# Four engines' order tables of a graph network kernel, made anew around VectorE's and GpSimd's shared port

## What is computed

```python
x = _layernorm(x + L0(x))     # adj @ (x @ W) + b
x = _layernorm(x + L1(x))     # (si + sj + adj * w_r + g_b) @ x @ W + b
x = _layernorm(x + L2(x))     # attention: e = sigmoid(a_tgt + a_src + be) * mask; elu twice
x = _layernorm(x + L3(x))     # 5 steps of a gated recurrent unit on adj @ h
```

## Time and profile before

| what | value |
|---|---|
| median of 3 runs (lowest, highest) | 1314.46 us (1313.87, 1315.95) |
| the profiled execution | 1314.02 us |
| its span, first to last instruction | 1312.2 us |
| mean granted clock of TensorE | 0.98 of full speed |
| share of the span: ACT busy | 45% |
| what TensorE does most: line 622, three kinds of matmul on `xh`, `xl` | 656 matmuls of each kind |

### The profile page before, as it was taken

The page is one execution under the profiler, slowest core; times in us unless marked ns, Lnnn a source line. Parts: engine busy times, 40 slices in busy tenths (PEclk is TensorE's granted clock), DMA queues, the critical chain, the costliest instruction groups (busy, mean ns, idle before and its releaser), DMA issues.

```text
span 1312.2 us, 15431 instructions
## 1 busy us (share of the span) xinstructions
PE 1232.6 (94%) x5488; PEld 938.1 (71%) x5488; DVE 921.8 (70%) x2154; ACT 587.1 (45%) x855; POOL 275.3 (21%) x174
## 2 busy tenths in 40 slices
PE   6968889999999999998999999999999999999994
...
DVE  6798767966866676669487666767677767655557
...
PEclk9977999999999999999999999999999999999997
...
DMA packets 38459, 52.70 MB, mean 40 GB/s; under 512 B 2736, under 2 KB 19632, under 8 KB 38384
## 3 DMA queue, kind: packets, MB, share of 16 engines
...
## 4 chain that ended last, share of the span: by engine, by line
PE 77%; DVE 15%; issue 3%; POOL 2%; ACT 2%; DMA 1%; POOLq 0%; SPq 0%; DVEq 0%; ACTq 0%
PE ps L622 41%; PE ps L627 6%; PE ps L629 6%; PE ps L628 6%; PE ps L719 5%; PE ps L633 4%; PE ps L640 3%; DVE x L1046 2%; DVE ring L1168 2%; PE ps L837 2%; DVE tl L1023 1%; PE ps L732 1%; PE ps L681 1%; PE ps L733 1%; PE ps L711 1%
## 5 line engine op out<-in xcount | busy, mean ns | idle before, releaser
L622 PE MATMUL ps<-adj_hi,xh 128*128 128x512 f32 x656 | 284.1, 433 | 4.1 <-DVE xl L1023 2.3
L622 PE MATMUL ps<-adj_hi,xl 128*128 128x512 f32 x656 | 257.1, 392 | 0.0
L622 PE MATMUL ps<-adj_lo,xh 128*128 128x512 f32 x656 | 256.2, 390 | 0.0
L622 PEld LDWEIGHTS ps<-adj_hi,xh 128*128 128x128 f32 x656 | 123.4, 188 | 41.9 <-issue 17.5
L591 POOL TENSOR_TENSOR fr<-fr,ring 128x512 f32<-128x512 f32 x84 | 126.9, 1511 | 104.9 <-DVE ring L1168 101.2
L622 PEld LDWEIGHTS ps<-adj_lo,xh 128*128 128x128 f32 x656 | 123.6, 188 | 34.3 <-issue 12.5
L622 PEld LDWEIGHTS ps<-adj_hi,xl 128*128 128x128 f32 x656 | 123.1, 188 | 27.0
L1168 DVE TENSOR_TENSOR ring<-ring,mk 128x512 f32<-128x512 f32 x128 | 104.7, 853 | 32.3 <-ACT ring L907 31.1
L719 PE MATMUL ps<-ring,fz 128*128 128x512 f32 x224 | 112.2, 610 | 15.8 <-DVE ring L1168 15.8
L1186 DVE TENSOR_TENSOR r<-r,hT 128x512 f32<-128x512 f32 x80 | 62.2, 789 | 92.0 <-ACT r L960 92.0
L863 ACT ACTIVATE mh<-ps 128x512 fp32r<-128x512 f32 x80 | 47.8, 597 | 172.8 <-PE ps L622 172.6
(11 more groups left out here) (272 smaller groups left out, 2486.0 us busy)
## 6 DMA issues: line engine op xcount, KB each, us to landing
mk<-mask_scratch SPq DMA_DIRECT2D x128, 256.0 KB, 2.8
...
```

Of the source, the lines that this page charges most:

```text
L622: mm = pe.matmul(dst, a[:, t, :], b[:, t, cut(h)], start=(t == 0 and i == 0), stop=(t == T - 1 and i == 2))
```

## The change

All instructions stay as they are, and so do the functions that issue them. Only the text of `TABLES` differs: the four orders are made anew, with the condition that in the plan VectorE and GpSimd never hold the SBUF port that they share at the same time. Besides the first stage, units 0, 1, 3, 4, 10 to 18 and 20 to 28 differ. Lines of the same kind are left out below (units 20 to 28 repeat 10 to 18 nearly; ScalarE's and VectorE's slots in those units move with TensorE's).

```diff
--- before.py
+++ after.py
...
     "PE": """
...
-first rows:0 y1a:0 m1b:1 y1b:0 sums:1 rows:1 y1a:1 y1b:1 t2a:0 t2b:0 t2a:1 t2b:1 pja:1 pja:0 pjb:0 pjb:1
-first tha:0 thb:0 tga:0 tgb:0 tha:1 thb:1 tga:1 e00:0 e01:0 e02:0 tgb:1 m1a:2 e03:0 e04:0 e05:0 e06:0 m1b:2
-first e07:0 sums:2 rsa:0 rows:2 y1a:2 rva:0 e10:0 e11:0 e12:0 y1b:2 y2a:0 e13:0 e14:0 e15:0 e16:0 e17:0
-first e00:1 rsb:0 m0a:3 rvb:0 e01:1 e02:1 e03:1 m0b:3 y2b:0 e04:1 e05:1 e06:1 y0a:3 y0b:3 e07:1 t2a:2 t2b:2
-first e10:1 e11:1 e12:1 pja:2 pjb:2
-unit0 @2 e13:1 e14:1 e15:1 tha:2 thb:2 @3 tga:2 tgb:2 e16:1 e17:1 @5 rsa:1 m1a:3 rsb:1 m1b:3 rva:1 sums:3 e00:2 e01:2 rows:3 y1a:3 rvb:1 y1b:3 e02:2 @6 e03:2 @7 y2a:1 e04:2 @8 y2b:1 e05:2 e06:2 @17 e07:2 @19 rsa:2 @21 rva:2 @25 e10:2 y2a:2 e11:2 e12:2 e13:2
-unit1 @10 e14:2 @26 e15:2
+first rows:0 y1a:0 m1b:1 y1b:0 sums:1 rows:1 y1a:1 t2a:0 t2b:0 pja:0 pjb:0 y1b:1 tha:0 thb:0 tga:0 tgb:0
+first m1a:2 m1b:2 e00:0 e01:0 e02:0 sums:2 e03:0 e04:0 e05:0 t2a:1 t2b:1 rows:2 y1a:2 e06:0 e07:0 pja:1
+first y1b:2 rsa:0 rva:0 e10:0 e11:0 pjb:1 e12:0 y2a:0 e13:0 e14:0 e15:0 tha:1 e16:0 thb:1 tga:1 tgb:1 e17:0
+first rsb:0 m0a:3 rvb:0 e00:1 e01:1 e02:1 m0b:3 y2b:0 e03:1 e04:1 e05:1 y0a:3 y0b:3 e06:1 e07:1 t2a:2 t2b:2
+first pja:2 pjb:2 e10:1
+unit0 @1 e11:1 e12:1 @5 e13:1 tha:2 thb:2 @6 e14:1 e15:1 tga:2 tgb:2 @8 e16:1 e17:1 rsa:1 @12 rsb:1 m1a:3 rva:1 m1b:3 rvb:1 sums:3 e00:2 y2a:1 rows:3 y1a:3 y2b:1 e01:2 y1b:3 e02:2 @19 e03:2 @25 e04:2
+unit1 @1 e05:2 e06:2 @2 e07:2 @4 rsa:2 e10:2 e11:2 rva:2 @7 e12:2 @10 y2a:2 @19 e13:2 @22 e14:2 @26 e15:2
...
-unit13 @2 y0b:5 @9 e00:4 e01:4 e02:4 @11 e03:4 e04:4 @14 e05:4 e06:4 @16 e07:4 @18 rsa:4 @20 rva:4 e10:4 e11:4 e12:4 m1a:5 @21 y2a:4 e13:4 @22 e14:4 @23 e15:4 @25 e16:4 @27 e17:4
-unit14 @2 m1b:5 @14 rsb:4 @16 rvb:4 @19 sums:5 @23 y2b:4 @27 rows:5
...
+unit13 @2 m0b:5 tha:4 thb:4 y0a:5 tga:4 tgb:4 @5 y0b:5 @7 e00:4 e01:4 e02:4 @10 e03:4 e04:4 @20 e05:4 e06:4 @21 e07:4 @24 rsa:4 @27 rva:4 e10:4 e11:4 e12:4
+unit14 @7 y2a:4 e13:4 e14:4 e15:4 @8 m1a:5 e16:4 e17:4 @10 rsb:4 @11 m1b:5 @16 rvb:4 @19 sums:5 @23 y2b:4 @27 rows:5
...
-unit17 @2 e00:5 @7 e01:5 e02:5 @9 e03:5 e04:5 e05:5 @12 e06:5 e07:5 @14 rsa:5 e10:5 e11:5 rva:5 e12:5 e13:5 e14:5 @16 y2a:5 e15:5 e16:5 e17:5 @18 rsb:5 @20 rvb:5 @25 y2b:5
-unit18
+unit17 @2 e00:5 @7 e01:5 e02:5 @10 e03:5 e04:5 @18 e05:5 @20 e06:5 e07:5 @23 rsa:5 e10:5 e11:5 rva:5 e12:5 e13:5 e14:5 @25 y2a:5 e15:5 e16:5 @26 e17:5
+unit18 @1 rsb:5 @3 rvb:5 @9 y2b:5
...
-unit27 @1 rsa:7 e10:7 @2 rva:7 @4 e11:7 e12:7 @5 y2a:7 e13:7 e14:7 e15:7 @6 e16:7 @7 e17:7 @9 rsb:7 @16 rvb:7 @22 y2b:7
...
+unit27 @8 e06:7 e07:7 @10 rsa:7 e10:7 @16 rva:7 e11:7 e12:7 @17 e13:7 @19 y2a:7 e14:7 e15:7 e16:7 @21 e17:7 @23 rsb:7 @25 rvb:7
...
     "ACT": """
-first x0:0 x0:1 x0:2 m0a:0 m0b:0 m0a:1 m0b:1 weights:0 m0a:2 n0:0 m0b:2 m1a:0 n0:1 m1b:0 m1a:1 m1b:1 t2a:1
-first t2b:1 t2a:0 t2b:0 pja:1 pja:0 pjb:0 pjb:1 tha:0 thb:0 tga:0 tgb:0 tha:1 n0:2 thb:1 s00:0 s01:0 s02:0
-first tga:1 s03:0 s04:0 s05:0 tgb:1 m1a:2 s06:0 s07:0 m1b:2 x0:3 e07:0 s10:0 s11:0 s12:0 rva:0 s13:0 s14:0
-first s15:0 s16:0 s17:0 s00:1 e17:0 s01:1 s02:1 s03:1 m0a:3 rvb:0 s04:1 s05:1 s06:1 m0b:3 s07:1 e07:1 s10:1
-first s11:1 s12:1
...
+first x0:0 x0:1 x0:2 weights:0 m0a:0 m0b:0 m0a:1 m0b:1 m0a:2 n0:0 m0b:2 m1a:0 n0:1 m1b:0 m1a:1 m1b:1 n0:2
+first t2a:0 t2b:0 pja:0 pjb:0 tha:0 thb:0 tga:0 tgb:0 s00:0 s01:0 s02:0 m1a:2 s03:0 s04:0 m1b:2 s05:0 x0:3
+first s06:0 s07:0 t2a:1 t2b:1 e07:0 s10:0 s11:0 pja:1 s12:0 rva:0 s13:0 s14:0 s15:0 pjb:1 s16:0 s17:0 tha:1
+first thb:1 tga:1 tgb:1 e17:0 s00:1 s01:1 s02:1 m0a:3 rvb:0 s03:1 s04:1 s05:1 m0b:3 s06:1 s07:1 e07:1 s10:1
+first s11:1 t2a:2 s12:1 t2b:2 pja:2
...
     "DVE": """
-first x0:0 x0:1 x0:2 weights:0 y0a:0 y0b:0 y0a:1 v0:0 y0b:1 mask:0 n0:0 v0:1 l1:0 d1:0 n0:1 mask:1 l1:1 d1:1
-first sums:0 mask:2 y0a:2 mask:3 rows:0 mask:4 y1a:0 mask:5 y1b:0 sums:1 v1:0 rows:1 n1:0 y1a:1 y1b:1 mask:6
-first v1:1 mask:7 n1:1 y0b:2 v0:2 pja:1 pja:0 pjb:0 pjb:1 n0:2 as:0 as:1 s00:0 s01:0 s02:0 l1:2 d1:2 s03:0
-first s04:0 s05:0 s06:0 s07:0 sums:2 rsa:0 s10:0 s11:0 s12:0 rows:2 rva:0 y1a:2 s13:0 s14:0 s15:0 y2a:0
-first y1b:2 v1:2 s16:0 s17:0 s00:1 n1:2 x0:3 s01:1 s02:1 rsb:0 s03:1 rvb:0 s04:1 s05:1 s06:1 y2b:0 v2:0
-first s07:1 y0a:3 y0b:3 n2:0 s10:1 s11:1 s12:1
-unit0 @0 v0:3 s13:1 s14:1 s15:1 pja:2 pjb:2 n0:3 s16:1 s17:1 as:2 l1:3 d1:3 rsa:1 s00:2 s01:2 s02:2 rsb:1 sums:3 rva:1 rows:3 s03:2 y1a:3 rvb:1 y1b:3 s04:2 v1:3 y2a:1 s05:2 @1 s06:2 @2 y2b:1 n1:3 v2:1 s07:2 @4 n2:1 rsa:2 s10:2 s11:2 s12:2 rva:2 @9 y2a:2 s13:2
-unit1 @0 s14:2 s15:2 s16:2 @5 s17:2
...
+first x0:0 x0:1 x0:2 weights:0 mask:0 mask:1 mask:2 y0a:0 mask:3 y0b:0 y0a:1 v0:0 y0b:1 mask:4 n0:0 v0:1
+first l1:0 d1:0 n0:1 mask:5 l1:1 d1:1 sums:0 mask:6 y0a:2 mask:7 rows:0 y0b:2 y1a:0 v0:2 y1b:0 v1:0 sums:1
+first n0:2 n1:0 rows:1 pja:0 pjb:0 y1a:1 y1b:1 l1:2 as:0 v1:1 s00:0 s01:0 s02:0 d1:2 n1:1 s03:0 s04:0 s05:0
+first sums:2 s06:0 s07:0 rows:2 rsa:0 s10:0 s11:0 pja:1 s12:0 y1a:2 y1b:2 rva:0 s13:0 v1:2 y2a:0 s14:0 s15:0
+first pjb:1 s16:0 n1:2 s17:0 as:1 x0:3 rsb:0 s00:1 s01:1 s02:1 rvb:0 s03:1 s04:1 s05:1 y2b:0 v2:0 s06:1
+first s07:1 y0a:3 y0b:3 n2:0 s10:1
+unit0 @0 s11:1 s12:1 v0:3 pja:2 s13:1 pjb:2 s14:1 s15:1 n0:3 s16:1 s17:1 as:2 @2 rsa:1 l1:3 d1:3 rsb:1 s00:2 s01:2 s02:2 rva:1 rvb:1 sums:3 y2a:1 rows:3 y2b:1 y1a:3 v2:1 y1b:3 s03:2 v1:3 @4 n2:1 n1:3 @9 s04:2
+unit1 @0 s05:2 s06:2 s07:2 s10:2 s11:2 rsa:2 s12:2 s13:2 s14:2 rva:2 s15:2 @5 y2a:2 @6 s16:2 @7 s17:2
...
     "POOL": """
-first x0:0 x0:1 x0:2 n0:0 n0:1 n1:0 n1:1 pjb:1 pjb:0 n0:2 s01:0 s02:0 s03:0 s04:0 s05:0 s06:0 s07:0 s11:0
-first s12:0 s13:0 s14:0 s15:0 n1:2 s16:0 s17:0 x0:3 s01:1 s02:1 s03:1 s04:1 s05:1 s06:1 n2:0 s07:1 s11:1
-first s12:1 pjb:2 s13:1 n0:3 s14:1 s15:1 s16:1 s17:1 s01:2 s02:2 s03:2 s04:2 n1:3 s05:2 s06:2 n2:1 s07:2
+first x0:0 x0:1 x0:2 n0:0 n0:1 n0:2 n1:0 pjb:0 n1:1 s01:0 s02:0 s03:0 s04:0 s05:0 s06:0 pjb:1 s07:0 s11:0
+first s12:0 s13:0 n1:2 s14:0 s15:0 s16:0 s17:0 x0:3 s01:1 s02:1 s03:1 s04:1 s05:1 n2:0 s06:1 s07:1 pjb:2
+first s11:1 s12:1 n0:3 s13:1 s14:1 s15:1 s16:1 s17:1 s01:2 s02:2 n2:1 s03:2 n1:3 s04:2 s05:2 s06:2 s07:2
...
```

More of the change, by code:

```diff
@@ L47 @@
 unit9
-unit10 @22 m0a:4 @24 m0b:4 @26 y0a:4
-unit11 @1 y0b:4 @25 m1a:4 @27 m1b:4
-unit12 @2 sums:4 @4 rows:4 @8 y1a:4 @11 y1b:4 @26 t2a:4 t2b:4 m0a:5 pja:4 pjb:4 m0b:5 tha:4 thb:4 y0a:5 tga:4 tgb:4
-unit13 @2 y0b:5 @9 e00:4 e01:4 e02:4 @11 e03:4 e04:4 @14 e05:4 e06:4 @16 e07:4 @18 rsa:4 @20 rva:4 e10:4 e11:4 e12:4 m1a:5 @21 y2a:4 e13:4 @22 e14:4 @23 e15:4 @25 e16:4 @27 e17:4
-unit14 @2 m1b:5 @14 rsb:4 @16 rvb:4 @19 sums:5 @23 y2b:4 @27 rows:5
+unit10 @21 m0a:4 @26 m0b:4
+unit11 @1 y0a:4 @3 y0b:4 @25 m1a:4 @27 m1b:4
@@ L53 @@
+unit12 @2 sums:4 @4 rows:4 @8 y1a:4 @11 y1b:4 @26 t2a:4 t2b:4 @27 pja:4 pjb:4 m0a:5
+unit13 @2 m0b:5 tha:4 thb:4 y0a:5 tga:4 tgb:4 @5 y0b:5 @7 e00:4 e01:4 e02:4 @10 e03:4 e04:4 @20 e05:4 e06:4 @21 e07:4 @24 rsa:4 @27 rva:4 e10:4 e11:4 e12:4
+unit14 @7 y2a:4 e13:4 e14:4 e15:4 @8 m1a:5 e16:4 e17:4 @10 rsb:4 @11 m1b:5 @16 rvb:4 @19 sums:5 @23 y2b:4 @27 rows:5
 unit15 @6 y1a:5 @21 y1b:5
 unit16 @6 t2a:5 t2b:5 @7 pja:5 pjb:5 @11 tha:5 @20 thb:5 tga:5 @21 tgb:5
-unit17 @2 e00:5 @7 e01:5 e02:5 @9 e03:5 e04:5 e05:5 @12 e06:5 e07:5 @14 rsa:5 e10:5 e11:5 rva:5 e12:5 e13:5 e14:5 @16 y2a:5 e15:5 e16:5 e17:5 @18 rsb:5 @20 rvb:5 @25 y2b:5
```

88 lines of the change are left out of this document (46 added, 42 removed).

## The result

| | before | after |
|---|---|---|
| median, same chip, in turn | 1315.2 us | 1276.15 us (1275.51 to 1276.34) |
| the profiled execution | 1314.02 us | 1275.51 us |
| its span | 1312.2 us | 1273.7 us |

The account below looks back on a forecast made before the run. TensorE was taken as the bound, with the stake in its idle time and half clock. The forecast was 1314.0 - 12 (36 to 160) - 2 (units 0 and 1) - 6 (pairs 2 and 3) = 1294 us, range 1278 to 1315.

Parts of the forecast that it names:

- What bounds the kernel: Whole kernel: TensorE bounds it, busy 1232.6 of 1312.2 us; nothing to win from 310 to 575 and 1080 to 1290.
- Weights, masks and gate: First stage: earlier `weights` lets masks end at 70.4 instead of 96.5; first tile product at about 101 instead of 118.11.
- The tile stage of batch 0: Its 16 tiles take the same 42 us; VectorE's lead falls from 17.1 to 12; -12 us for 36 to 160.
- My sign for this: TensorE's idle time from 36 to the end of unit 1 falls from 34.7 to about 20 us.
- Units 0 and 1: From 160 to 310: tiles spread in unit 0 but crowded in unit 1; -2 us, ends +5 and -9.
- Pairs 2 and 3: 575 to 760 and 888 to 1080: wider tile spacing cuts waits for tile products; -6 us, ends +6 and -12.
- The port: SBUF port of VectorE and GpSimd: nothing counted for port time removed; VectorE's busy 921.8 us falls by less than 30.
- The first (1304): Early gain alone: unit 1 costs 2 us more than unit 0 saves, later idle time stays; 1304 us, chance 0.24.
- The second, the slow clock: Batch 0's tile stage stays at 1.2 GHz, costing 18 us more; 1320 us, chance 0.10.
- The third: No change: the 12 us ahead turn into idle time again before unit 0; 1314 us, chance 0.10.
- The fourth, all lower ends at 1276 us: Lower ends reached in all three places, 1314 - 17 - 9 - 12 = 1276 us; chance 0.06.

Follow-up runs that it names:

- run 3: Kernel before with only ScalarE's `weights` in front of `m0a:0` and VectorE's eight masks at their new places: 1310.65 us, ratio 0.9978.
- Run 12: Changed kernel with the product `m1:2` put back among the tiles of batch 0 on TensorE, ScalarE and VectorE: 1284.84 us, ratio 0.9782.
- run 5: Kernel before with GpSimd's row sum additions on 8 columns instead of 512, the rest of each row sum left out: 1284.51 us, ratio 0.9771.
- run 6: Changed kernel with GpSimd's row sum additions on 8 columns instead of 512, the rest of each row sum left out: 1274.31 us, ratio 0.9698.
- run 2: Old tables up to unit 9, new tables from unit 10 on: 1295.38 us, ratio 0.9856 against the kernel before.

## Why the prediction was right and wrong

**What bounds the kernel: right.** 310 to 575 and 1080 to 1290 gained nothing, and the whole gain lies in the three stretches with idle time. Of the 19 us between forecast and profile, about 1 is the loads, 5 the tile stage of batch 0 and 12 pairs 2 and 3.

**Weights, masks and gate: right in time, wrong in credit.** The last mask came 1.2 us before its forecast, the first tile product 1.0, about what the earlier loads gave. But run 3 gives 3 us for this step alone: in the old order it only moves the wait.

**The tile stage of batch 0: the step that failed first.** I had VectorE 17.1 us ahead at the first tile product (18.1 measured, 1 of it the loads), and then charged 6.4 - 1.2 = 5.2 us for `pja:1 pjb:1 n1:1 as:1`, put off into the tile stage, as if VectorE set that stage's pace. It didn't: in the old order it stood there for 8.6 us in one wait for `sums:2`, behind `m1b:2`. With `m1:2` ahead of the tiles that wait is gone, the stage is as long as before (46.6 us, before 164.90 - 118.11 = 46.8), and the put-off work lies in it for nothing: VectorE is busy for 42.8 us of it, before for 35.7. ("Within 1 us" of the old load, as I had summed, was wrong too.) Run 12 shows it from the other side, with the wait back and 6.7 us lost in that stage. I had read VectorE's 29.9 of 41 us busy and compared loads, but not asked what the 11 idle us waited for. Measured for 36 to 160: -18.3, or -17.4 without the loads, forecast -12. My sign for this, idle time of about 20 us up to unit 1, came out at 20.2 all the same. That is luck: TensorE's busy time fell by another 5 us, which I hadn't counted, by less half clock (some 3 us, the estimate above) and by hidden waits.

**Units 0 and 1: right.** -2 forecast, -1.9 measured (18.3 to 20.2).

**Pairs 2 and 3: right place, wrong size.** -6 forecast with a lower end of -12, -18 measured (10.0 and 8.2). This is the larger miss. I took the waits for tile products, 5.5 + 4.4 us, as the stake and somewhat over half of them as the gain. Two things were missed: nearly all idle time went (15.6 to 2.6), and another 5 us that stood in no wait, hidden in TensorE's busy time (2.5 in each pair). So my lower end, 12 us, lay inside the 15.6 us of idle time, and the stake was larger still than the idle time. What showed in its place is the port: with small additions and the old order, these two pairs gain 15.5 of the 18 us (run 5).

**The port: half right.** "VectorE's busy total falls by less than 30" holds, it rose by 3. That the tables can't keep the two apart on the chip holds as well, by the line of the tile products in the changed kernel:

```profile
L1168 DVE TENSOR_TENSOR ring<-ring,mk x128: 672/686/2068, 100.0 to 1014.4; 128x512 f32<-128x512 f32 x128
```

The longest is 2068 ns, 1785 before, and VectorE's holds add up to 57 us in both orders (runs 5 and 6). (GpSimd wasn't silent for the whole 1.92 us that I read at 118.11: its first addition starts at 119.56, during the third product.) What was wrong is the conclusion "I count nothing for port time removed". I had written myself that a gain can come only from what waits for the port, and then priced nobody who waits. Holds cost the old order 30 us (run 5), some 13 of them before unit 2, and the new order 2. So in pairs 2 and 3 the change earned its name in another sense than it is meant: it doesn't remove the holds, it makes them fall where nobody waits. There the holds and the spacing of the tiles are in the main one cause and not two, since most of the waits that spacing was to relieve vanish as well when GpSimd's additions are short; the new order is worth 3 us more even then (pairs 2 and 3 gain 15.5 us in run 5 and 18.6 in run 6). Before unit 2 it isn't shown: there the change wins ahead of the first tile product, and the holds cost the old order behind it.

**The rivals.** The first (1304), with only the early gain, is excluded by run 2: the late half alone brings 1.4%. Its sign, `ml` among the longest waits, does stand in pair 3 with one wait of 1.5 us, but only because hardly any other wait is left. The second, the slow clock, went the other way: `m1:2` ahead of the tiles filled the stretch, and from 92 to 106 the granted clock is 1.00, where it was 0.69 from 92 to 119; over the tiles of batch 0 (106 to 146) it is 0.96, where this rival needed about 0.5. The third is excluded by the result. The fourth, all lower ends at 1276 us, hit the number with terms 20, and 18 where it had 26 and 12; that it fits is luck. I gave it 0.06 and cut most of it out of the range. Its low chance came from treating the three ends as independent. As I now read runs 5 and 12, each hangs on how much room VectorE has, so they would be reached together; that is argued, not shown.
